# One signal of TensorE per expert tile, two banks and a third weight buffer in a fused attention and mixture-of-experts block

## The chip, the cores and the metric

The kernel runs on one core of a Trainium2 chip. The metric is the device time of one execution in microseconds; the kernel before has a median of 491.53 over three runs (491.47 to 492.46). On a core five engines run their own instruction streams: TensorE (PE, with its weight loads as PEld), VectorE (DVE), ScalarE (ACT), GpSimd (POOL) and SyncE (SP). They meet only at semaphores: an instruction adds one when it is done, another waits until a count is reached. SP, ACT and POOL also issue DMAs.

## What is computed

The block takes 16 sequences of 256 positions with 128 features. A modulated layer norm feeds a linear attention with a state that is updated position by position (the scan), its result is gated and added to the input; a second modulated layer norm feeds a mixture of eight experts, of which each position takes one:

```python
h = _layernorm(x, axis=-1) * (1 + ca) + sa
x = x + ga * _L0_attn_ref(h, ...)          # the scan over 256 positions
h = _layernorm(x, axis=-1) * (1 + cb) + sb
x = x + gb * _L0_ffn_ref(h, ...)
...
logits = x @ router_w + router_b
max_ind = jnp.argmax(route, axis=1)
for e in range(num_experts):               # 8 experts
    a, g = jnp.split(x @ w1[e], 2, axis=1) # 128 -> 2 x 512
    y = jax.nn.silu(a) * g @ w2[e]         # 512 -> 128
    out = jnp.where((max_ind == e)[:, None], y, out)
out = out * max_prob
```

## The kernel before

The positions are cut in two halves of 128. Up to about 300 us the scan runs on DVE, with the other engines beside it. The first half's rows go through the router while the scan of the second half still runs; the second half's only after it.

The experts' stage is what the change touches. For each half POOL scatters the 2048 normed rows into a DRAM array sorted by expert (`sort_rows`, L996, 16 indirect DMAs of 128 rows each, in three bursts of 6, 5 and 5, each burst waiting for the one before it to land). The sorted rows form 23 tiles of 128 rows with one expert each (`NF = 23`), so 46 tiles, g = 0 to 45. What each engine does for a tile:

- SP loads the tile's rows (L534), after the whole half has been scattered.
- PE turns the rows (`turn_x`, L827, one product against the identity, into bank 0), makes the first products in two halves of eight (`hidden`, L839), and two tiles later the second products, eight (`second`, L854, into bank 3). Its loop over g is: first half of `hidden(g)`, `turn_x(g + 2)`, second half of `hidden(g)`, `second(g - 2)`.
- DVE copies the turned rows to SBUF (`xst`, L1886) and their places (L1888), multiplies (`gate_u`, L1893), and from tile 13 on copies the result (`ys`, L1900).
- ACT applies the silu (L1386), copies the next but one tile's first weights into one of two buffers (`copy_w1`, L1399), and up to tile 12 copies the result (`ys`, L1406).
- POOL scatters the result rows (L1052), after tile 10 stops for the second half's `sort_rows` (`SCAT = 10`), and then goes on with tile 11.

Every order is written out by hand. PE counts four kinds of event apart: `xt_ps` for each turn, `h_ps` for each half of `hidden`, `y_ps` for each `second`. So it signals four times in a tile. The silu starts at the first half's signal, `xst` at the turn's, `copy_w1` at the second half's.

While tiles 3 to 15 run, other work of the second half is woven in: PE adds `attend` (L710) behind tiles 3 and 4, turns of normed rows (L729) behind 8 and 10, router products and turns back (L738, L747) behind 9 and 11, and the ranks (L755) behind 12. On DVE, behind `xst` of the same iteration, stand the statistics, the scaling, `shift2` (L1796, eight instructions at 9 and 11, which PE's router products wait for), the routing (L1727 to L1739 at 12, which the ranks wait for) and the sorted places (L1759 to L1785 at 13, which POOL's `sort_rows` waits for). `scale_outputs` (L246) follows `gate_u` in iterations 0 and 1; ACT sends what the first one made by four DMAs (L259) before it copies tile 3's weights.

## Time and profile before

| what | us |
|---|---|
| median of the runs (lowest, highest) | 491.53 (491.47, 492.46) |
| span of the profiled execution, first to last instruction | 487.9 |
| PE busy in the span | 377.1 (77%) |
| DVE busy | 383.3 (79%) |
| ACT busy | 277.9 (57%) |
| POOL busy | 263.1 (54%) |
| chain that ended last, by engine | DVE 33%, PE 31%, POOL 13%, issue 11% |
| mean granted TensorE clock | 0.886 of full speed |

For the profiled execution only its span is known; the median of the runs is 3.6 us above it. The page's second part cuts the span in 40 slices: PE shows 9 in nearly all of the slices from 404 us to 470 us, and in that stretch the chain that ended last is PE's products, tile after tile. From 370 us to 404 us the same chain is broken by pieces called "issue" and "another core or an unknown queue", that is, time for which the profile shows no releaser or one that it can't name. Before 300 us the chain is DVE's scan.

### The profile page before, as it was taken

The page shows a single profiled execution, that of the slowest core. Times are in us where ns is not written, and L with a number is a line of the kernel's source. Part 1 is how long each engine was busy: PE and PEld are TensorE (multiplying, and loading weights), DVE is VectorE, ACT ScalarE, POOL GpSimd, SP SyncE. Part 2 cuts the span into 40 slices and gives each one's busy share as a digit, 9 for nine tenths or more (in the row PEclk, how much of TensorE's full clock was granted, in tenths as well). Part 3 has the DMA queues.
Part 4 walks back from the last instruction along what each step waited for, and adds up shares of the span by engine and source line. Part 5 has one row for each costly group of instructions (what it writes and reads, how often), then busy time and mean ns, then how long its engine had stood idle before and what let it go on. Part 6 is the DMA issues. An engine that isn't in the chain of part 4 may idle for free.

```text
span 487.9 us, 8633 instructions
## 1 busy us (share of the span) xinstructions
PE 377.1 (77%) x2505; PEld 325.1 (67%) x2505; DVE 383.3 (79%) x1166; ACT 277.9 (57%) x624; POOL 263.1 (54%) x325
## 2 busy tenths in 40 slices
PE   2967763956799978948779588699997779999970
PEld 1322312754678568938669578598997678999960
DVE  5778999999999999999979997749664224468624
ACT  3697967756474666766466353548454354555520
POOL 1127238999999678576772884022216663333340
PEclk9978995978889997987976869989999977999995
DMA  8177799990000019431000011341131122414006
GB/s 227 41 101 125 109 118 151 103 69 1 1 0 1 2 18 388 114 57 31 0 2 0 13 39 51 75 88 35 39 114 38 50 78 56 130 42 130 29 27 177
DMA packets 49309, 35.00 MB, mean 72 GB/s; under 512 B 10992, under 2 KB 45584, under 8 KB 49136
## 3 DMA queue, kind: packets, MB, share of 16 engines
q1 hardware_dynamic: 45424, 28.28, 30.7%
q0 software_dynamic: 3264, 5.92, 4.0%
q8 instruction: 21, 0.34, 0.3%
q10 hardware_dynamic: 576, 0.26, 0.2%
q14 instruction: 24, 0.20, 0.2%
HBM read 15.26 MB, written 10.27 MB: 52 GB/s over the span
## 4 chain that ended last, share of the span: by engine, by line
DVE 33%; PE 31%; POOL 13%; issue 11%; ACT 5%; DMA 2%; another core or an unknown queue 2%; ACTq 1%; SPq 0%; POOLq 0%; DVEq 0%
PE bank L839 12%; PE bank L854 5%; DVE U L1682 5%; DVE S L1695 5%; DVE p L1676 4%; DVE p L1689 4%; PE bank L650 4%; POOL big L950 2%; DVE big L1612 2%; PE bank L738 2%; DVE X L1614 2%; PE bank L593 1%; PE bank L654 1%; POOL X L918 1%
## 5 line engine op out<-in xcount | busy, mean ns | idle before, releaser
L1052 POOL DMA_INDIRECT placed_y<-Q,place x46 | 44.1, 958 | 101.9 <-DVE place L1888 38.1
L839 PE MATMUL bank<-Q,p 128*128 128x128 f32 x736 | 97.2, 281 | 2.2 <-ACT p L1399 2.2
L650 PE MATMUL bank<-prod_o,ID 128*128 128x128 f32 x512 | 75.4, 308 | 29.0 <-POOL prod_o L294 17.1
L839 PEld LDWEIGHTS bank<-Q,p 128*128 128x128 f32 x736 | 92.1, 197 | 2.6 <-ACT p L1399 2.4
L650 PEld LDWEIGHTS bank<-prod_o,ID 128*128 128x128 f32 x512 | 70.4, 219 | 31.8 <-POOL prod_o L294 20.3
L1210 ACT ACTIVATE p<-S,GAM 128x64 f32<-128x64 f32 x126 | 48.3, 410 | 65.4 <-DVE S L1695 64.6
L287 POOL TENSOR_TENSOR prod_o<-Q,ST 128x1024 f32<-128x1024 f32 x28 | 60.0, 2141 | 29.6 <-PE bank L654 17.1
L1399 ACT ACTIVATE p<-big 128x1024 f32 x46 | 48.5, 1057 | 44.4 <-PE bank L839 30.7
L1695 DVE TENSOR_REDUCE S<-p 128x64 f32<-128x320 f32 x126 | 56.6, 488 | 0.0
L1682 DVE TENSOR_REDUCE U<-p 128x32 f32<-128x288 f32 x128 | 53.0, 454 | 0.0
L1676 DVE TENSOR_TENSOR p<-S,bank 128x256 f32<-128x256 f32 x128 | 49.7, 423 | 0.7 <-ACT bank L1205 0.7
L1689 DVE TENSOR_TENSOR p<-U,bank 128x256 f32<-128x256 f32 x126 | 48.4, 423 | 0.0
L854 PE MATMUL bank<-big,S 128*128 x248 | 34.7, 284 | 9.6 <-issue 4.6
L996 POOL DMA_INDIRECT sorted_h<-X,pos x32 | 30.9, 965 | 18.6 <-issue 8.1
L593 PE MATMUL bank<-ph,WP 128*128 128x512 f32 x48 | 29.9, 772 | 13.4 <-ACT ph L1098 13.4
L854 PEld LDWEIGHTS bank<-big,S 128*128 128x128 f32 x248 | 30.7, 195 | 11.3 <-issue 11.2
L1893 DVE TENSOR_TENSOR S<-S,bank 128x512 f32<-128x512 f32 x31 | 21.3, 687 | 19.1 <-PE bank L839 11.0
L654 PEld LDWEIGHTS bank<-prod_o,ID 128*128 128x128 f32 x256 | 35.2, 213 | 0.0
L654 PE MATMUL bank<-prod_o,ID 128*128 128x128 f32 (+3 forms) x256 | 34.7, 284 | 0.0
L1886 DVE COPY Q<-bank 128x128 f32<-128x128 f32 x46 | 13.3, 288 | 27.1 <-PE bank L827 21.7
L294 POOL TENSOR_TENSOR prod_o<-PD,U 128x128 f32<-128x128 f32 (+1 forms) x112 | 33.7, 339 | 0.0
L1386 ACT ACTIVATE S<-bank 128x512 f32<-128x512 f32 x31 | 18.5, 595 | 20.0 <-PE bank L839 10.0
(253 smaller groups left out, 740.4 us busy)
## 6 DMA issues: line engine op xcount, KB each, us to landing
big<-in_L_ffn_w_dram SPq DMA_DIRECT2D x1, 4096.0 KB, 14.1
big<-big SPq DMA_DIRECT2D x16, 192.0 KB, 5.0
Q<-sorted_h SPq DMA_DIRECT2D x46, 64.5 KB
sorted_h<-ZERO SPq DMA_DIRECT2D x2, 1472.0 KB, 19.4
X<-in_L_attn_x_dram SPq DMA_DIRECT2D x8, 256.0 KB, 4.4
big<-big SPq DMA_DIRECT2D x16, 128.0 KB, 5.2
K<-placed_y SPq DMA_DIRECT2D x8, 256.0 KB
out_dram<-X SPq DMA_DIRECT2D x8, 256.0 KB, 2.3
```

Of the source, the lines that this page charges most:

```text
L287: engine.tensor_tensor(slot[:, 0:HD, :, :, :], q, states.unsqueeze(3).broadcast_to(full), ALU.mult)
L650: pe.matmul(ps, ID[:, :], prod_o[:, k % 2, i, :], start=(i == 0), stop=False, skip_group_check=True)
L654: m = pe.matmul(o4, ID[:, :], r4, start=False, stop=(d == C - 1), skip_group_check=True)
L839: m = pe.matmul(bank[(1, 6)[g % 2] + k][:, c * P:(c + 1) * P], W1E[g % 2][:, f:f + P], XST[:, g % 3, :], start=True, stop=True)
L854: m = pe.matmul(bank[3][:, 0:D], GU[g % 3][:, c * P:(c + 1) * P], W2[:, bass.ds(expert, 1), c, :], start=(c == 0), stop=(c == FC - 1))
L1052: pool.indirect_dma_start(placed_y[g // NF], bass.IndirectOffsetOnAxis(ap=place[:, g:g + 1], axis=0), YS[:, g % YR, :], None).then_inc(sem ...
L1210: act.activation(p2[h][:, :, :, C], S_[h][:, n % SR, :, :], ACT.Copy, scale=GAM[h][:, n:n + 1])\
L1399: act.activation(W1E[g % 2].unsqueeze(1), W1[:, bass.ds(expert, 1), :], ACT.Copy).then_inc(sem("w1_copied"), 1)
L1676: dve.tensor_tensor(p1[h][:, n % UR, :, :, 0:HD], s_, w, ALU.mult).then_inc(sem("seq_w", h), 1)
L1682: dve.tensor_reduce(U_[h][:, n % VR, :, :], p1[h][:, n % UR, :, :, :], AX_X, ALU.add)\
L1689: dve.tensor_tensor(p2[h][:, :, :, 0:C], u, k, ALU.mult).then_inc(sem("state_in", h), 1)
L1695: dve.tensor_reduce(S_[h][:, (n + 1) % SR, :, :], p2[h][:, :, :, :], AX_X, ALU.add).then_inc(sem("s_ready", h), 1)
```

## The change

PE signals once per tile, at its last product, on one count `tile_ps`; `xt_ps`, `h_ps` and `y_ps` go. The helpers `hidden_done`, `result_done` and `turned` translate a tile to that count. From tile 17 on (`WIDE = 16`) turned rows alternate between banks 0 and 5 and results between banks 3 and 4, and PE waits for the copy of the last but one instead of the last. First weights get a third buffer from tile 8 on, and ACT copies them three tiles ahead from iteration 5 on, in which it copies two. DVE's `ys` moves from three iterations behind to two, and behind `xst`.

```diff
+        W1E.append(flatq[0][:, HB * P:HB * P + F2])
+        THREE, WIDE = 6, F_ROUTE + 4
+        def first_weights(g):
+            return W1E[g % 2 if g < THREE else (g - THREE) % 3]
+        def hidden_done(g):
+            return g + 3 if g < NF else g + 7
+        def result_done(g):
+            return g + 5 if g < NF else hidden_done(g + 2)
+        def turned(g):
+            if g < 2:
+                return g + 1
+            return g + 5 if NF <= g < NF + 2 else hidden_done(g - 2)
+        def turned_bank(g):
+            return bank[5 if g > WIDE and g % 2 else 0][:, 0:P]
+        def result_bank(g):
+            return bank[4 if g > WIDE and g % 2 else 3][:, 0:D]
...
             def turn_x(g):
                 pe.wait_ge(sem(f"xs_in{g % XR}"), 16 * (g // XR + 1))
                 if g >= 1:
-                    pe.wait_ge(sem("xst_ready"), g)
-                pe.transpose(bank[0][:, 0:P], XS[:, g % XR, 0:D], ID[:, :]).then_inc(sem("xt_ps"), 1)
+                    pe.wait_ge(sem("xst_ready"), g if g <= WIDE else g - 1)
+                if g == WIDE + 1:
+                    pe.wait_ge(sem("h2_evac"), 8)
+                return pe.transpose(turned_bank(g), XS[:, g % XR, 0:D], ID[:, :])
...
-                    m.then_inc(sem("h_ps"), 1)
                     if k == 0 and g + 2 < G and g + 2 not in (NF, NF + 1):
                         turn_x(g + 2)
+                return m
...
                 if g >= 1:
-                    pe.wait_ge(sem("ys_ready"), g)
+                    pe.wait_ge(sem("ys_ready"), g if g <= WIDE else g - 1)
+                if g == WIDE + 1:
+                    pe.wait_ge(sem("pos_ready"), 2)
...
-                m.then_inc(sem("y_ps"), 1)
+                return m
...
                 if g < G:
-                    hidden(g)
+                    last = hidden(g)
                 if g >= 2 and g not in (NF, NF + 1):
-                    second(g - 2)
+                    last = second(g - 2)
+                last.then_inc(sem("tile_ps"), 1)
...
             def silu(g):
-                act.wait_ge(sem("h_ps"), 2 * g + 1)
-                if g >= 3:
-                    act.wait_ge(sem("y_ps"), g - 2)
+                act.wait_ge(sem("tile_ps"), hidden_done(g))
...
-                if g >= 2:
-                    act.wait_ge(sem("h_ps"), 2 * (g - 1))
-                else:
+                if g < 2:
                     act.wait_ge(sem("u_ready", g), NCH)
+                if g == THREE + 2:
+                    act.wait_ge(sem("ot_in0_", 1), 16 * HB)
...
-                if g + 2 < G:
+                if g < THREE:
                     copy_w1(g + 2)
+                if THREE - 1 <= g and g + 3 < G:
+                    copy_w1(g + 3)
...
             def xst(g):
-                dve.wait_ge(sem("xt_ps"), g + 1)
-                if g >= 3:
-                    dve.wait_ge(sem("h_ps"), 2 * (g - 2))
-                dve.tensor_copy(XST[:, g % 3, :], bank[0][:, 0:P]).then_inc(sem("xst_ready"), 1)
+                dve.wait_ge(sem("tile_ps"), turned(g))
+                dve.tensor_copy(XST[:, g % 3, :], turned_bank(g)).then_inc(sem("xst_ready"), 1)
...
             def gate_u(g):
                 dve.wait_ge(sem("silu_a"), g + 1)
-                dve.wait_ge(sem("h_ps"), 2 * g + 2)
...
-                elif g >= YACT + 3 and g not in (NF + 1, NF + 2):
-                    if g == YACT + 3:
-                        dve.wait_ge(sem("ys_ready"), YACT)
-                    ys(g - 3)
                 if g + 2 < G and g + 2 not in (NF, NF + 1):
                     xst(g + 2)
+                if g >= YACT + 2 and g not in (NF, NF + 1):
+                    if g == YACT + 2:
+                        dve.wait_ge(sem("ys_ready"), YACT)
+                    ys(g - 2)
```

DVE's program around iterations 12 and 13 of the kernel before, with the semaphores that each instruction waits for: the multiply of tile 11, then the copy of tile 14's turned rows, and the start of the routing.

```order
L1893 TENSOR_TENSOR S<-S,bank 128x512 [waits h_ps,silu_a]
L1886 COPY Q<-bank 128x128 [waits h_ps,xt_ps]
L1888 CAST place<-Q 128x1 [waits xs_in0]
L1727 TENSOR_TENSOR RT<-bank,RB 128x128 [waits lg_ps]
L1732 TENSOR_REDUCE lmx<-RT 128x16 [waits dve_link]
```

The same place in the changed kernel:

```order
L1927 TENSOR_TENSOR S<-S,bank 128x512 [waits silu_a]
L1921 COPY Q<-bank 128x128 [waits tile_ps]
L1923 CAST place<-Q 128x1 [waits xs_in0]
L1763 TENSOR_TENSOR RT<-bank,RB 128x128 [waits lg_ps]
L1768 TENSOR_REDUCE lmx<-RT 128x16 [waits dve_link]
```

Nothing changes its place here; the copy of the turned rows, which stands ahead of the routing, now waits for the count of whole tiles.

DVE's program of iterations 16 and 17 before: multiply of tile 15, result of tile 13, turned rows of tile 18, multiply of 16, result of 14.

```order
L1893 TENSOR_TENSOR S<-S,bank 128x512 [waits h_ps,silu_a]
L1900 COPY Q<-bank 128x128 [waits ys_out0,y_ps,ys_ready]
L1886 COPY Q<-bank 128x128 [waits h_ps,xt_ps]
L1888 CAST place<-Q 128x1 [waits xs_in4]
L1893 TENSOR_TENSOR ST<-ST,bank 128x512 [waits h_ps,silu_a]
L1900 COPY Q<-bank 128x128 [waits ys_out1,y_ps]
```

And in the changed kernel, from the multiply of tile 15 on:

```order
L1927 TENSOR_TENSOR S<-S,bank 128x512 [waits silu_a]
L1921 COPY Q<-bank 128x128 [waits tile_ps]
L1923 CAST place<-Q 128x1 [waits xs_in4]
L1934 COPY Q<-bank 128x128 [waits ys_out1,tile_ps]
L1927 TENSOR_TENSOR ST<-ST,bank 128x512 [waits silu_a]
```

The result's copy now stands behind the turned rows, and it is one tile further on: `ys_out1` is tile 14's, one iteration earlier than before.

## Rows read from the trace of the kernel before

**Rows 1.** Busy time by stretch (engines' busy us, then PEclk, DMA share, GB/s).

```profile
369.70:404.70 35.00, 26.21 (x191) 24.65 (x190) 9.33 (x27) 15.29 (x18) 22.26 (x24) 0.90 0.19 58
391.00:394.00 3.00, 3.00 (x16) 3.00 (x16) 1.06 (x4) 2.04 (x3) 1.98 (x3) 0.50 0.45 114
```

**Rows 2.** Timeline of PE, tile 5 (start us, us, engine, line, operation, [idle before]).

```profile
328.40 1.06 PE L839 MATMUL bank<-Q,p 128*128 128x128 f32 x8
329.29 0.27 PE L827 MATMUL bank<-ID,Q 128*128 128x128 f32 x1
...
331.19 1.06 PE L839 MATMUL bank<-Q,p 128*128 128x128 f32 x8
```

**Rows 3.** Timeline of ACT and DVE in the same tile.

```profile
329.49 0.60 ACT L1386 ACTIVATE S<-bank 128x512 f32<-128x512 f32 x1 [1.73 <-PE bank L839]
329.60 0.29 DVE L1886 COPY Q<-bank 128x128 f32<-128x128 f32 x1 [1.35 <-PE bank L827]
...
333.00 0.69 DVE L1893 TENSOR_TENSOR S<-S,bank 128x512 f32<-128x512 f32 x1
```

**Rows 4.** Timeline of all engines during POOL's first burst, tiles 15 to 17.

```profile
366.71 0.96 POOL L996 DMA_INDIRECT sorted_h<-X,pos  x1 [4.60 <-DVE pos L1785]
...
370.61 0.27 PE L827 MATMUL bank<-ID,Q 128*128 128x128 f32 x1
...
373.02 0.96 POOL L996 DMA_INDIRECT sorted_h<-X,pos  x1 [0.31 <-issue]
...
374.55 1.15 PE L854 MATMUL bank<-big,S 128*128 x8 [2.77 <-issue]
...
375.43 0.60 ACT L1386 ACTIVATE ST<-bank 128x512 f32<-128x512 f32 x1 [2.75 <-remote]
375.47 0.29 DVE L1886 COPY Q<-bank 128x128 f32<-128x128 f32 x1 [1.18 <-remote]
```

**Rows 5.** Timeline during a burst of the first half's sort, before the experts' stage.

```profile
295.45 0.96 POOL L996 DMA_INDIRECT sorted_h<-X,pos  x1 [1.61 <-DMA sorted_h<-X,pos]
...
298.20 0.98 PE L654 MATMUL bank<-prod_o,ID 128*128 128x128 f32 x8
...
299.21 0.28 ACT L1240 ACTIVATE K<-bank 128x128 f32<-128x128 f32 x1 [3.77 <-PE bank L654]
```

**Rows 6.** Timeline of DVE, SP and PE: from places to the second half's first turn.

```profile
366.26 0.17 DVE L1785 CAST pos<-bank 128x16 uint32<-128x16 f32 x1
...
391.16 0.32 SPq L534 DMA_DIRECT2D Q<-sorted_h  x1
...
404.73 0.42 PE L827 MATMUL bank<-ID,Q 128*128 128x128 f32 x1
...
302.93 0.36 SPq L534 DMA_DIRECT2D Q<-sorted_h  x1
...
304.86 0.30 PE L827 MATMUL bank<-ID,Q 128*128 128x128 f32 x1
```

**Rows 7.** Timeline of PE and DVE: places in tiles 3 to 13 where PE waits.

```profile
317.52 1.16 PE L839 MATMUL bank<-Q,p 128*128 128x128 f32 x8 [2.25 <-ACT p L1399]
...
339.95 1.15 PE L854 MATMUL bank<-big,S 128*128 x8 [1.12 <-ACT Q L1406]
...
354.09 1.06 PE L738 MATMUL bank<-RW,K 128*128 128x8 f32 x8
...
360.56 0.49 PE L755 MATMUL bank<-RT,LOWER 128*128 128x128 f32 x2 [0.68 <-DVE RT L1739]
...
362.55 0.29 DVE L1886 COPY Q<-bank 128x128 f32<-128x128 f32 x1 [1.45 <-PE bank L827]
```

**Rows 8.** Timeline of PE: tile 20 and the last products.

```profile
389.83 1.37 PE L854 MATMUL bank<-big,S 128*128 x8 [1.86 <-issue]
...
469.23 1.06 PE L854 MATMUL bank<-big,ST 128*128 x8
...
472.62 1.15 PE L854 MATMUL bank<-big,S 128*128 x8 [0.59 <-DVE Q L1900]
```

More of the change, by code:

```diff
@@ L838, in hidden @@
                         f = (k * FC + c) * P
-                        m = pe.matmul(bank[(1, 6)[g % 2] + k][:, c * P:(c + 1) * P], W1E[g % 2][:, f:f + P], XST[:, g % 3, :],
+                        m = pe.matmul(bank[(1, 6)[g % 2] + k][:, c * P:(c + 1) * P], first_weights(g)[:, f:f + P], XST[:, g % 3, :],
                                       start=True, stop=True)
-                    m.then_inc(sem("h_ps"), 1)
                     if k == 0 and g + 2 < G and g + 2 not in (NF, NF + 1):
                         turn_x(g + 2)
+                return m
             def second(g):
@@ L851, in second @@
                 if g >= 1:
-                    pe.wait_ge(sem("ys_ready"), g)
+                    pe.wait_ge(sem("ys_ready"), g if g <= WIDE else g - 1)
+                if g == WIDE + 1:
+                    pe.wait_ge(sem("pos_ready"), 2)
                 for c in range(FC):
-                    m = pe.matmul(bank[3][:, 0:D], GU[g % 3][:, c * P:(c + 1) * P], W2[:, bass.ds(expert, 1), c, :],
+                    m = pe.matmul(result_bank(g), GU[g % 3][:, c * P:(c + 1) * P], W2[:, bass.ds(expert, 1), c, :],
                                   start=(c == 0), stop=(c == FC - 1))
-                m.then_inc(sem("y_ps"), 1)
+                return m
             for g in range(2):
-                turn_x(g)
+                turn_x(g).then_inc(sem("tile_ps"), 1)
             for g in range(G + 2):
@@ L862, in _ @@
                     for k in (2, 1):
-                        second(g - k)
+                        second(g - k).then_inc(sem("tile_ps"), 1)
                     for k in range(2):
-                        turn_x(g + k)
+                        turn_x(g + k).then_inc(sem("tile_ps"), 1)
                 if g < G:
-                    hidden(g)
+                    last = hidden(g)
                 if g >= 2 and g not in (NF, NF + 1):
-                    second(g - 2)
+                    last = second(g - 2)
+                last.then_inc(sem("tile_ps"), 1)
                 if g in F_ATTEND:
@@ L1393, in copy_w1 @@
                     act.wait_ge(sem("tex_ready"), s + 1)
-                if g >= 2:
-                    act.wait_ge(sem("h_ps"), 2 * (g - 1))
-                else:
+                if g < 2:
                     act.wait_ge(sem("u_ready", g), NCH)
+                if g == THREE + 2:
+                    act.wait_ge(sem("ot_in0_", 1), 16 * HB)
                 expert = act.value_load(tex[s][0:1, j:j + 1], min_val=0, max_val=E - 1)
-                act.activation(W1E[g % 2].unsqueeze(1), W1[:, bass.ds(expert, 1), :], ACT.Copy).then_inc(sem("w1_copied"), 1)
+                act.activation(first_weights(g).unsqueeze(1), W1[:, bass.ds(expert, 1), :], ACT.Copy).then_inc(sem("w1_copied"), 1)
             def ys(g):
-                act.wait_ge(sem("y_ps"), g + 1)
+                act.wait_ge(sem("tile_ps"), result_done(g))
                 if g >= YR:
                     act.wait_ge(sem(f"ys_out{g % YR}"), 16 * (g // YR))
-                act.activation(YS[:, g % YR, :], bank[3][:, 0:D], ACT.Copy).then_inc(sem("ys_ready"), 1)
+                act.activation(YS[:, g % YR, :], result_bank(g), ACT.Copy).then_inc(sem("ys_ready"), 1)
             for h in range(NHALF):
@@ L1896, in ys @@
             def ys(g):
-                dve.wait_ge(sem("y_ps"), g + 1)
+                dve.wait_ge(sem("tile_ps"), result_done(g))
                 if g >= YR:
                     dve.wait_ge(sem(f"ys_out{g % YR}"), 16 * (g // YR))
-                dve.tensor_copy(YS[:, g % YR, :], bank[3][:, 0:D]).then_inc(sem("ys_ready"), 1)
+                dve.tensor_copy(YS[:, g % YR, :], result_bank(g)).then_inc(sem("ys_ready"), 1)
             def finish(s, q):
@@ L1923, in _ @@
             xst(1)
-            for g in range(G + 3):
+            for g in range(G + 2):
                 if g == NF:
-                    for k in (3, 2, 1):
+                    for k in (2, 1):
                         ys(g - k)
```

## Prediction

> **What bounds the kernel now.** I read the chain that ended last first. From 404 us on it is PE's products, one tile after another, up to the scatters and stores of the end; between 370 and 404 us it breaks into pieces without a known releaser. Then the busy times by stretch: from 369.7 to 404.7 us PE is busy 26.2 of 35.0 us [rows 1]. The timeline of an undisturbed tile says what this stretch should take. Tile 5 begins at 328.40, its turn at 329.29, tile 6 at 331.19 [rows 2]: eight products take 0.89 us, the turn 0.11, a whole tile (24 products and the turn) 2.79. The stretch holds tiles 16 to 22, two of them without a turn, and two second products: 7 × 2.79 − 0.22 + 1.78 = 21.1 us. So 13.9 of the 35.0 us are lost there, to waits and to half clock.
>
> The timelines of all engines show what the waits are. In tile 5 ACT begins its silu at 329.49 and DVE its copy at 329.60, each 0.20 us after the last product that it needs [rows 2, 3]. In tile 16 the first half ends at 370.61 and the turn at 370.72, but ACT's silu and DVE's copy start together at 375.43 and 375.47 [rows 4], some 4.7 us late, and neither waits for anything else in the program that is still running. PE itself then waits 2.77 us, because the result that DVE has to copy was late in the same way. POOL was issuing six indirect DMAs back to back, from 366.71 to 373.98; the two start 1.5 us after the last. The same pattern comes back in the next three bursts. I take it that PE's signals arrive late while POOL issues in bursts. But not always: in a burst of the first half's sort, running since 295.45, PE ends its eight products of L654 at 298.20 + 0.89 = 299.1, and ACT follows at 299.21 [rows 5]. There PE signals once in 24 products, here four times in 25. So what fits both is that signals pile up when they are close together. This is an inference, not something that a row says.
>
> A second path runs beside PE's. The places of the second half are ready at 366.26 + 0.17 = 366.43; POOL's sixteen scatters follow, and SP loads the first sorted tile at 391.16, which is 24.73 us later [rows 6]. In the first half the turn came 304.86 − 302.93 = 1.93 us after that load. So tile 23's turn could have stood at 393.09; PE, held up, came to it at 404.73. There are 11.6 us between what the sort allows and what PE did.
>
> **The change, part by part.** *One signal per tile.* In tiles 16 to 22 signals then come 2.79 us apart, about as far as in rows 5. I count these waits as gone, with 1.9 us of cover left in any case: the silu of tile g is needed at the start of tile g + 2, 2.79 us after the signal, and takes 0.20 + 0.60 [rows 3].
>
> *The price of the one signal.* DVE's copy of turned rows moves from the turn's end to the tile's end, from 329.40 to 331.19 [rows 2], or 1.79 us. Whatever stands behind that copy on DVE and is waited for by PE or POOL moves as well:
> - Tile 0 has no second products, so there the move is one group of eight, 0.89. Behind the copy stand the square roots, `gate_u`, `scale_outputs`, then ACT's four DMAs and the copy of tile 3's weights, for which PE already waits 2.25 us [rows 7]: +0.89.
> - Iteration 5: from the copy at 329.60 DVE works without a gap on the statistics; ACT's root and result copy follow, and PE already waits 1.12 us for that at 339.95 [rows 7]: +1.79. The wait that ACT's two weight copies in iteration 5 make for PE a tile or two earlier (about 1 us) lies inside this.
> - Iterations 9 and 11: PE's router products began at 354.09 with no idle time worth a note beside the row [rows 7], just as the first four of DVE's `shift2` were done; with 0.1 us of slack that is +1.7 each, 3.4 in all.
> - Iteration 12: the ranks already wait 0.68 us for DVE's routing [rows 7]: +1.79.
> - Iteration 13: the copy at 362.55 [rows 7] stands ahead of the sorted places: +1.79.
>
> The places are then 0.89 + 1.79 + 3.4 + 1.79 + 1.79 = 9.7 us later, at 376.1, and tile 23's turn at 376.1 + 24.73 + 1.93 = 402.8. PE gets there sooner: it begins tile 15's second half at 377.0, when the multiply behind the places (0.69 [rows 3]) is done, ends tile 15 two groups later at 378.8, and with 21.1 us of work and 0.9 of waiting for the last multiply ends both second products at 400.8. So 2 us of delays could return there for nothing, and the sort is the bound. Against 404.73: −1.9.
>
> *Two banks.* After the turn of tile 23 the next turn no longer waits for DVE's copy (−0.3), two short waits of some 0.2 us each while DVE runs the first half's end go (−0.4), and at the very end the last second products, which wait 0.59 at 472.62 after a like wait just before, start when the multiply is done: tile 45 ends at 469.23 + 0.89 = 470.12 [rows 8], +0.20, silu 0.60, multiply 0.69 [rows 3], +0.2 is 471.8, so −0.8. Together −1.5. In tiles 25 to 43 PE already runs without a gap, so the banks give nothing there.
>
> *The third buffer* lets the weights arrive a tile earlier; where PE runs gap-free nothing waits for them, so nothing. *Fewer signals on PE:* the turn follows a signalled product 0.11 us after the group's end, as any product follows another [rows 2], so nothing. The Trainium skill, in "TensorE: Matmul & The Clock Gate", section "The cost: per-tile semaphore tail", gives some 26 ns to each increment and says that one on the last product is enough. By that the 138 signals that go would be worth an estimated 3.6 us, and the sum would be that much lower; tile 5's rows show no such time.
>
> *The clock.* From 391 to 394 us the granted clock is 0.50, the lower of TensorE's two levels (1.2 and 2.4 GHz), and 16 products fill 3.0 us [rows 1] instead of 1.8: 1.2 us lost there, and 1.7 over the whole fall, which began a little earlier. It followed PE's 1.86 us wait at 389.83 [rows 8], yet not the longer one of 2.77 us at 374.55 [rows 4]. The change makes three new waits of this length before the places, 1.8 in iterations 9 and 11 and 2.5 at the ranks. Between no fall and three (0 to 5.1 us) I take one: +1.7.
>
> **The sum.** −1.9 − 1.5 + 1.7 = −1.7 us on the span of 487.9, which gives 486.2. The median of the runs is 3.6 us above that span, and I keep this distance: 491.53 − 1.7 = **489.8**.
>
> **The rivals.** A measurement of this kernel can tell about 0.2%, 1 us, from no change.
>
> *Signals are held by the burst itself* (slower). If POOL's back-to-back issue holds any signal of PE until it pauses, then one signal per burst passes, and PE, two tiles deep, does two tiles per burst. A burst and its pause took about 7.5 us, so 3.8 us a tile: tiles 16 to 22 and the second products end at 378.8 + 28 = 407, or 4 us after the sort's bound, and while POOL then works off the waiting results for some 16 us, four tiles lose 1 us each. 489.8 without the clock term is 488.1; plus 8 is 496. For it: the late starts fall 1 to 1.5 us after bursts. Against it: rows 5. It decides as soon as signals arrive more than 1.9 us late.
>
> *The clock falls at every new wait* (slower). 491.53 − 3.4 + 5.1 = 493.2. For it: the wait of 1.86 us; against: the one of 2.77.
>
> *The early waits are partly hidden* (faster). If ACT or DVE have more slack in iterations 5 to 13 than the rows of PE's waits show and only half of the 9.7 us appears, the turn of tile 23 moves to 398 and the time to about 484. Against it: at each of these places PE or POOL already waits, or is within 0.1 us of waiting.
>
> *Signals cost PE time* (faster). If each signal that goes gave PE back its spacing, the time would fall further; rows 2 are rounded to 0.01, so three signals in 46 tiles can give at most 1.4 us: 488.4. This is what the page's rule would come to here.
>
> **How the numbers follow.** The forecast, with no fall of the clock (488.1), one (489.8) or two (491.5), has 0.60, 0.20 each. Held signals 0.18, three falls 0.12, half the early waits 0.07, signals that cost 0.03. Faster by over 0.2% are the first two of the forecast and the last two rivals: 0.40 + 0.07 + 0.03 = 0.50. Same is the third of the forecast, 0.20. Slower are the held signals and three falls, 0.30. The forecast's own range is 487 to 492. The 8-in-10 range runs from 486.5, which leaves out the hidden waits, to 496, up to the held signals at their price.
>
> **What would show it.** Right: in the second half's sort, silu and copy start about 0.2 us after a tile's end; PE's router products, twice, and the ranks wait some 2 us; the places come near 376 us, SP's first load near 401, tile 23's turn near 403, and that turn waits for the load, not for PE. The last second products follow a wait for the multiply, not for a result's copy. Wrong: starts that still come a microsecond after a burst; a turn of tile 23 that follows PE's products without a wait; places before 372 or after 380 us.

## The result and the profile after

The changed kernel takes 502.81 us (median of four runs, 500.54 to 506.5) against 491.5 for the kernel before: 1.0267 of its time, interval 1.0219 to 1.0314. It is slower by 11.3 us; I had forecast 1.7 us less, and a range that ended at 496.0.

The profiled execution of after has a span of 498.8 us and a time of 500.54; that of before 487.9. The difference of the spans, 10.9 us, is what the two traces have to account for. Every reading below is of one profiled execution per kernel.

The page of after, its first part and two groups of its fifth (busy us, mean ns of one | idle us before, and what ended most of it):

```profile
span 498.8 us, 8511 instructions
PE 379.7 (76%) x2505; PEld 327.3 (66%) x2505; DVE 382.1 (77%) x1166; ACT 277.9 (56%) x624; POOL 263.3 (53%) x325
...
L1921 DVE COPY Q<-bank 128x128 f32<-128x128 f32 x46 | 13.3, 289 | 65.2 <-PE bank L888 50.7
...
L1420 ACT ACTIVATE S<-bank 128x512 f32<-128x512 f32 x31 | 18.5, 596 | 49.0 <-PE bank L888 40.8
```

The same two groups on the page of before:

```profile
L1886 DVE COPY Q<-bank 128x128 f32<-128x128 f32 x46 | 13.3, 288 | 27.1 <-PE bank L827 21.7
...
L1386 ACT ACTIVATE S<-bank 128x512 f32<-128x512 f32 x31 | 18.5, 595 | 20.0 <-PE bank L839 10.0
```

The work is the same to within 3 us on each engine. What grew is idle time: DVE is now idle for 65.2 us ahead of its copies of turned rows where it was idle for 27.1, and 50.7 us of that end with the last product of a tile; ahead of ACT's silu it is 49.0 us where it was 20.0. In before some of that idle time was no loss to anybody, so the groups alone don't say what the program lost. That stands in PE's timeline, at the places of [rows 7]. After, PE, tiles 3 to 13, rows with a wait of over 1 us, and the next tile's products behind the last three:

```profile
320.14 1.16 PE L871 MATMUL bank<-Q,p 128*128 128x128 f32 x8 [2.24 <-ACT p L1433]
...
330.60 2.02 PE L739 MATMUL bank<-ph,X 128*128 128x128 f32 x16 [1.20 <-DVE X L1755]
...
338.50 1.15 PE L888 MATMUL bank<-big,ST 128*128 x8 [1.20 <-ACT Q L1440]
...
346.36 1.15 PE L888 MATMUL bank<-big,S 128*128 x8 [1.50 <-ACT Q L1440]
...
352.89 1.06 PE L767 MATMUL bank<-RW,K 128*128 128x8 f32 x8 [1.72 <-DVE K L1832]
...
356.67 1.92 PE L871 MATMUL bank<-Q,p 128*128 128x128 f32 x8
...
366.06 1.06 PE L767 MATMUL bank<-RW,K 128*128 128x8 f32 x8 [1.72 <-DVE K L1832]
...
368.90 1.74 PE L871 MATMUL bank<-Q,p 128*128 128x128 f32 x8
...
375.95 0.79 PE L784 MATMUL bank<-RT,LOWER 128*128 128x128 f32 x2 [2.46 <-DVE RT L1775]
...
377.01 1.89 PE L871 MATMUL bank<-Q,p 128*128 128x128 f32 x8
```

In before the same stretch shows three waits, 2.25, 1.12 and 0.68 us [rows 7]. Soon after each of the last three waits a row of eight products takes 1.7 to 1.9 us instead of 1.06. Busy time by stretch of after shows why (columns as in [rows 1]; the clock stands before the DMA share):

```profile
357.00:358.30 1.30, 1.30 (x8) 1.30 (x8) 0.00 (x0) 0.52 (x1) 0.00 (x0) 0.50 0.00 0
369.20:370.40 1.20, 1.20 (x7) 1.20 (x7) 0.00 (x0) 0.50 (x1) 0.00 (x0) 0.50 0.00 0
...
377.20:378.60 1.40, 1.40 (x8) 1.40 (x8) 0.00 (x0) 0.00 (x0) 0.00 (x0) 0.50 0.88 351
```

The granted clock is 0.50, the lower level of 1.2 GHz. In before it was full throughout:

```profile
340.00:366.70 26.70, 26.02 (x224) 25.24 (x225) 17.76 (x62) 13.42 (x23) 5.72 (x6) 1.00 0.23 70
```

The second path, from the places to the second half's first turn, in after (DVE, POOL, SP and PE):

```profile
384.81 0.17 DVE L1821 CAST pos<-bank 128x16 uint32<-128x16 f32 x1
...
385.26 0.96 POOL L1031 DMA_INDIRECT sorted_h<-X,pos  x1 [8.54 <-DVE pos L1821]
...
409.22 2.70 SPq L563 DMA_DIRECT2D Q<-sorted_h  x6
...
418.27 0.64 PE L859 MATMUL bank<-ID,Q 128*128 128x128 f32 x2
```

Counted from the stage's first turn (306.61, and 304.86 before), the places are ready after 78.37 us instead of 61.57: 16.8 later. The load follows them by 24.2 us, before by 24.7 [rows 6]. But tile 23's turn follows the load by 9.05 us, not by 1.93, and without any wait for it: PE came late. A burst shows what held it. After, second half's sort, ACT, PE, POOL and DVE around the end of the first burst:

```profile
387.85 0.60 ACT L1420 ACTIVATE S<-bank 128x512 f32<-128x512 f32 x1 [1.58 <-issue]
...
389.54 1.06 PE L888 MATMUL bank<-big,S 128*128 x8
...
391.58 0.96 POOL L1031 DMA_INDIRECT sorted_h<-X,pos  x1 [0.30 <-issue]
393.89 0.60 ACT L1420 ACTIVATE ST<-bank 128x512 f32<-128x512 f32 x1 [4.20 <-remote]
393.89 0.29 DVE L1921 COPY Q<-bank 128x128 f32<-128x128 f32 x1 [4.04 <-remote]
...
394.70 1.15 PE L888 MATMUL bank<-big,S 128*128 x8 [2.10 <-DVE Q L1934]
```

The signal of the tile that ended at 387.64 arrived in 0.21 us. The next tile ended at 389.54 + 0.89 = 390.43; ACT and DVE saw it together at 393.89, 3.46 us later and 1.35 us after POOL's last issue of the burst ("remote" stands for a releaser that the profile can't name). The longest delays in the other two bursts are 2.90 and 3.92 us. So one signal per tile is held like four. PE's busy time from the first indirect DMA to tile 23's turn, before and after:

```profile
366.71:404.73 38.02, 29.23 (x219) 27.67 (x217) 11.76 (x36) 17.04 (x21) 24.67 (x26) 0.90 0.19 57
...
385.26:418.27 33.01, 25.30 (x207) 24.09 (x206) 11.48 (x36) 15.20 (x20) 21.07 (x22) 0.98 0.19 57
```

PE is idle for 7.7 us there instead of 8.8. Most of the 5.0 us by which this piece is shorter is busy time: PE starts it about 12 products further on, and the granted clock is 0.98 instead of 0.90.

The end is as forecast in kind. After, PE, last products:

```profile
473.75 1.06 PE L871 MATMUL bank<-Q,p 128*128 128x128 f32 x8
...
476.54 1.95 PE L871 MATMUL bank<-Q 128*128 128x128 f32 x16
...
483.58 1.15 PE L888 MATMUL bank<-big,S 128*128 x8 [0.62 <-DVE S L1927]
```

The last wait is for the multiply, and a tile still takes 476.54 - 473.75 = 2.79 us. From tile 23's turn to POOL's last scatter it is 67.1 us instead of 69.7: 2.6 gained. The account: the stage began 1.75 us later (nothing of the change lies before it; it is the spread of runs), 16.8 later places, 418.27 - 384.98 = 33.3 us from there to the turn instead of 38.3 (-5.0), -2.6 at the end: 10.95, and the spans differ by 10.9.

### The profile page after: what moved, and what is told of

Its sections match the earlier page's. It is cut to its first block and busy times, and to the rows that moved or that the text cites. A ratio compares the mean times of both kernels' runs of the same rounds, so it can differ in the third digit from the quotient of the medians.

```text
span 498.8 us, 8511 instructions
## 1 busy us (share of the span) xinstructions
PE 379.7 (76%) x2505; PEld 327.3 (66%) x2505; DVE 382.1 (77%) x1166; ACT 277.9 (56%) x624; POOL 263.3 (53%) x325
## 5 line engine op out<-in xcount | busy, mean ns | idle before, releaser
L679 PEld LDWEIGHTS bank<-prod_o,ID 128*128 128x128 f32 x512 | 70.4, 219 | 33.0 <-POOL prod_o L323 21.6
L871 PE MATMUL bank<-Q,p 128*128 128x128 f32 x528 | 72.3, 287 | 4.4 <-ACT p L1433 2.2
L871 PEld LDWEIGHTS bank<-Q,p 128*128 128x128 f32 x528 | 68.2, 203 | 5.1 <-ACT p L1433 2.4
L1921 DVE COPY Q<-bank 128x128 f32<-128x128 f32 x46 | 13.3, 289 | 65.2 <-PE bank L888 50.7
L1712 DVE TENSOR_TENSOR p<-S,bank 128x256 f32<-128x256 f32 x128 | 48.5, 407 | 0.7 <-ACT bank L1240 0.7
L1725 DVE TENSOR_TENSOR p<-U,bank 128x256 f32<-128x256 f32 x126 | 47.3, 407 | 0.0
L622 PE MATMUL bank<-ph,WP 128*128 128x512 f32 x48 | 32.0, 821 | 14.6 <-ACT ph L1133 14.5
L1433 ACT ACTIVATE p<-big 128x1024 f32 x33 | 34.7, 1056 | 7.2 <-issue 6.3
L888 PE MATMUL bank<-big,S 128*128 x248 | 33.6, 278 | 5.0 <-DVE Q L1934 2.1
L683 PEld LDWEIGHTS bank<-prod_o,ID 128*128 128x128 f32 x256 | 36.4, 219 | 0.0
L683 PE MATMUL bank<-prod_o,ID 128*128 128x128 f32 (+3 forms) x256 | 35.9, 290 | 0.0
L622 PEld LDWEIGHTS bank<-ph,WP 128*128 128x128 f32 x48 | 11.7, 261 | 30.8 <-ACT ph L1133 16.5
```

Of the source, the lines that this page charges most:

```text
L622: m = pe.matmul(bank[1 + i][:, :], WP[:, i, :], rhs, start=True, stop=True)
L679: pe.matmul(ps, ID[:, :], prod_o[:, k % 2, i, :], start=(i == 0), stop=False, skip_group_check=True)
L683: m = pe.matmul(o4, ID[:, :], r4, start=False, stop=(d == C - 1), skip_group_check=True)
L871: m = pe.matmul(bank[(1, 6)[g % 2] + k][:, c * P:(c + 1) * P], first_weights(g)[:, f:f + P], XST[:, g % 3, :], start=True, stop=True)
L888: m = pe.matmul(result_bank(g), GU[g % 3][:, c * P:(c + 1) * P], W2[:, bass.ds(expert, 1), c, :], start=(c == 0), stop=(c == FC - 1))
L1712: dve.tensor_tensor(p1[h][:, n % UR, :, :, 0:HD], s_, w, ALU.mult).then_inc(sem("seq_w", h), 1)
```

## The experiments

Two questions: is the loss made before the places or after, and what holds the signals? The table has, for each kernel, three pieces of its trace: from the stage's first turn to the first indirect DMA of the second half's sort (A), from there to tile 23's turn (B), and from that turn to POOL's last scatter (C); beside B stand PE's idle time and the mean granted clock in it. Times are medians in us; "before" is the kernel before on the same chip, the ratio has its 95% interval.

| kernel | A | B | idle in B | clock in B | C | time | before | ratio |
|---|---|---|---|---|---|---|---|---|
| before | 61.9 | 38.0 | 8.8 | 0.90 | 69.7 | 491.5 | | |
| changed | 78.7 | 33.0 | 7.7 | 0.98 | 67.1 | 502.81 | 491.5 | 1.0267 (1.0219 to 1.0314) |
| late14 | 60.3 | 34.6 | 7.2 | 0.97 | 66.9 | 482.89 | 488.95 | 0.9878 (0.9796 to 0.9961) |
| four_banks | 61.9 | 30.1 | 3.4 | 1.00 | 68.1 | 481.85 | 488.95 | 0.9860 (0.9784 to 0.9936) |
| one_nobanks | 77.9 | 36.6 | 10.5 | 0.94 | 68.6 | 503.99 | 488.95 | 1.0296 (1.0215 to 1.0376) |
| late14_pre | 65.2 | 28.1 | 1.4 | 1.00 | 72.6 | 487.63 | 488.95 | 0.9973 (0.9934 to 1.0012) |
| turn14 | 62.7 | 40.9 | 11.6 | 0.87 | 67.6 | 492.60 | 494.74 | 0.9970 (0.9936 to 1.0005) |
| late14_reads | 62.7 | 34.8 | 6.9 | 0.94 | 67.5 | 486.84 | 494.74 | 0.9866 (0.9793 to 0.9939) |
| late14_narrow | 61.9 | 41.7 | 15.7 | 0.87 | 70.8 | one run | 494.74 | |
| late14_threes | 61.9 | 31.0 | 6.2 | 0.94 | 71.8 | 486.21 | 494.74 | 0.9839 (0.9780 to 0.9899) |
| turn14_threes | 64.2 | 31.0 | 5.7 | 0.96 | 70.8 | 487.71 | 493.38 | 0.9895 (0.9861 to 0.9929) |
| late14_fours | 61.9 | 29.3 | 3.9 | 1.00 | 68.5 | 479.95 | 493.38 | 0.9739 (0.9664 to 0.9814) |
| four_fours | 60.2 | 28.5 | 3.3 | 1.00 | 68.7 | 480.44 | 493.38 | 0.9766 (0.9686 to 0.9847) |
| before_threes | 61.9 | 32.7 | 7.2 | 0.97 | 74.8 | 487.82 | 493.38 | 0.9890 (0.9818 to 0.9962) |

The kernel before differs by 1.2% between the sets, so kernels of different sets are compared by ratio. A, B and C come from one execution each. Kernels with the same program up to the places (late14, late14_threes and late14_fours) have an A of 60.3 to 61.9: in late14 the granted clock stayed full at tile 3, where it fell to the lower level in the other two. It stayed full there in turn14 and four_fours as well, and fell in before and changed. In the kernels with bursts of three, 4.9 to 5.3 us of the idle time in B are the wait for the load.

### Where the loss is made

**late14** keeps the four signals up to iteration 13 (`LATE = 14`). The core of the edit (the waits on the other engines follow it):

```diff
+                    if g < LATE:
+                        m.then_inc(sem("h_ps"), 1)
...
+                        if g < LATE:
+                            r.then_inc(sem("xt_ps"), 1)
...
-                last.then_inc(sem("tile_ps"), 1)
+                if g >= LATE:
+                    last.then_inc(sem("tile_ps"), 1)
+                elif g >= 2:
+                    last.then_inc(sem("y_ps"), 1)
```

> The changed kernel, but with the four signals of before in iterations 0 to 13 of TensorE's loop, one per tile from 14 on; banks, third buffer and the order of the result copies as changed. Theory A (the loss is made before the places: DVE's copy of turned rows, held back to the tile's end, delays all that stands behind it): the places come as early as before, PE's waits at the router products and ranks go back to 0 to 0.7 us, and from the first indirect DMA to tile 23's turn it takes the 33.0 us of the changed kernel (38.0 before): 491.5 - 5.0 - 2.6 (tail) = 484, range 482 to 487. Theory B (the loss comes from what the change does from tile 14 on: banks, order of the copies, signals held in POOL's bursts): no better than 497.

**four_banks** is the same with `LATE = 1000`: four signals to the end, so only banks, third buffer and the earlier result copy are left of the change.

> Four signals per tile throughout, as before; only the two banks each, the third weight buffer and the earlier result copy of the change are kept. Theory A: places as early as before, PE held in POOL's bursts as before (38 us from the first indirect DMA to tile 23's turn, less up to 2 where the second bank lets PE run ahead), tail 1.5 to 2.6 shorter: 487 to 490. Theory B: some of the loss is here, 493 or more.

**one_nobanks** keeps the one signal and the earlier result copy, without the banks and the third buffer:

```diff
-        THREE, WIDE = 6, F_ROUTE + 4
+        THREE, WIDE = 1000, 1000
```

> One signal per tile as changed, but one bank each for turned rows and results and two weight buffers throughout. Theory A: the places are as late as in the changed kernel (about 385 us), the tail is 1.5 to 2.6 us longer: 503 to 506. Theory B (banks or third buffer cost the time): under 498.

Theory A holds in all three: with one signal before the places the kernel is 3% slower, banks or no banks; without it, it is 1.2 to 1.4% faster than before. In late14 A falls from 78.7 to 60.3 us, and PE waits 0.68 us for the ranks and not at all at the router products. The banks, the buffer and the earlier result copy together are worth 1.4% (interval 0.6 to 2.2%); I had expected 0.3 to 0.9%, with up to 2 us in the bursts, where B falls by 8, from 38.0 to 30.1 us: 5.4 us less idle time, the rest at a granted clock of 1.00 instead of 0.90. One signal instead of four from tile 14 on shows no gain over that.

**turn14** asks which waiter makes the loss. Everything waits for the tile's end as changed, but up to iteration 13 the turn signals as well, and DVE's copy waits for that (`TURNS = 14`):

```diff
+                        if g < TURNS:
+                            r.then_inc(sem("xt_ps"), 1)
...
-                dve.wait_ge(sem("tile_ps"), turned(g))
+                if g - 2 < TURNS:
+                    dve.wait_ge(sem("xt_ps"), g + 1)
+                    if g >= 3:
+                        dve.wait_ge(sem("tile_ps"), g - 2)
```

> The changed kernel with one signal more: up to iteration 13 the turn signals by itself too, and DVE's copy of turned rows waits for that; everything else waits for the tile's end as changed. Theory A1 (as the prediction had it: DVE's copy of turned rows is what makes the loss before the places): places 60 to 62 us after the stage's first turn, as before (changed kernel 78.4), time as with four signals up to iteration 13, 481 to 485. Theory A2 (the silu, the result's copy and the weight copies, which start at the tile's end as well, share in the loss): places after more than 64 us, 487 or more.

The places come 62.4 us after the first turn: A1 in the main. But in this trace the clock did not fall at tile 3, as it did in before and in changed. In turn14_threes (below), whose program is the same up to the places, it did, and there the places come after 63.9 us. Like for like, 78.4 - 63.9 = 14.5 of the 16.8 us belong to the one copy that stands ahead of other work on DVE, with the falls of the clock that follow it. The late silu and result copies, which still make PE wait for the results of tiles 4 to 6 (1.20, 0.25 and 1.50 us), have the other 2.3, the share that A2 spoke of. The time that A1 gave did not come either: B took 40.9 us, more than in any other kernel of full rows. From iteration 14 on its program is late14's, yet PE is idle for 11.6 us there instead of 7.2, and the granted clock is lower. late14 and turn14, B:

```profile
365.27:399.88 34.61, 27.40 (x219) 25.85 (x218) 11.62 (x36) 16.42 (x21) 22.40 (x24) 0.97 0.19 58
...
369.67:410.57 40.90, 29.30 (x222) 27.73 (x222) 11.74 (x36) 16.42 (x21) 25.16 (x27) 0.87 0.18 54
```

What differs is where its tiles end in the bursts. turn14, second burst, which began at 378.58, and the end:

```profile
380.56 1.06 PE L891 MATMUL bank<-big,S 128*128 x8
...
383.64 0.96 POOL L1037 DMA_INDIRECT sorted_h<-X,pos  x1 [0.30 <-issue]
385.90 0.60 ACT L1431 ACTIVATE S<-bank 128x512 f32<-128x512 f32 x1 [4.96 <-remote]
...
386.71 1.65 PE L891 MATMUL bank<-big,ST 128*128 x6 [3.19 <-DVE Q L1962]
```

A tile ended at 381.45, and its signal was seen at 385.90; PE waited 3.19 us. So the way through the bursts looks like a lottery: with one signal per tile it takes 28 to 41 us in kernels whose tile 15 begins between 1.05 us before the first indirect DMA (changed) and 1.0 after it (late14_pre below).

### What holds the signals

**late14_pre** reads the experts of tiles 14 to 22 into registers ahead of the bursts, since PE's own register reads could be what the bursts hold up:

```diff
+                if g == 12:
+                    for i in range(14, 23):
+                        pe_expert[i] = pe.value_load(tex[0][0:1, i:i + 1], min_val=0, max_val=E - 1)
```

> As the kernel with four signals up to iteration 13, and TensorE reads the experts of tiles 14 to 22 into registers in iteration 12, before POOL's bursts, instead of one ahead of each tile's second products. Theory H1 (POOL's back-to-back indirect DMAs by themselves hold PE's signals): ACT and DVE still start 2 to 4 us late in the bursts, time within 1.5 us of the kernel without the early reads. Theory H2 (PE's register read is held up by the bursts, and its signals behind it; in the first half's bursts, where PE reads no register, signals pass within 0.25 to 0.7 us): starts 0.2 us after a tile's end, tile 23's turn set by the sort, 26.7 us after the places: 5 to 7 us faster than that kernel.

Undecided by the time: the reads in one place made the ranks wait 4.40 us, so the sort began later, and B was the shortest of all (28.1). The signals were late all the same, by up to 2.87 us, but PE was idle for only 1.4 us in B; C is 5.7 us longer than late14's. **late14_reads** spreads them over waits of tiles 0 to 3:

```diff
+                if g == 3:
+                    read_experts(range(18, 23))
...
+                    if k == 0 and g in (0, 2):
+                        read_experts(range(14 + g, 16 + g))
```

> Four signals up to iteration 13, one from 14 on; TensorE reads the experts of tiles 14 to 22 into registers in waits that it has anyway, in tiles 0 to 3 (two, two and five reads). The first try of this, with all nine reads in iteration 12, made the ranks wait 4.4 us, but shortened the way from the first indirect DMA to tile 23's turn from 34.6 to 28.1 us. H2 (register reads in the bursts hold TensorE's signals): places as early as with four signals, 28 us to the turn: 475 to 479. H1 (the bursts by themselves): 33 us or more, 481 to 485.

B is 34.8 us, as in late14, and a signal is up to 4.46 us late: H2 falls. late14_pre's short B was then, as far as one trace tells, luck of the same lottery. late14_reads, PE in the bursts:

```profile
382.31 1.15 PE L901 MATMUL bank<-big,ST 128*128 x8 [1.41 <-issue]
...
391.28 3.37 PE L878 MATMUL bank<-Q,p 128*128 128x128 f32 x16 [1.95 <-issue]
```

**late14_narrow** scatters one number per row into an array of its own; the second half's experts then work on padding rows.

```diff
-                    pool.indirect_dma_start(sorted_h[s], bass.IndirectOffsetOnAxis(ap=pos[s][:, t:t + 1], axis=0),
-                                            H2[s][t // HB][:, t % HB, :], None).then_inc(sem("scattered", s), 16)
+                    c = slice(0, 1) if s else slice(0, D1)
+                    pool.indirect_dma_start(narrow if s else sorted_h[s], bass.IndirectOffsetOnAxis(ap=pos[s][:, t:t + 1], axis=0),
+                                            H2[s][t // HB][:, t % HB, c], None).then_inc(sem("scattered", s), 16)
```

> Four signals up to iteration 13, one from 14 on; the second half's sort scatters one number of each row (4 bytes) instead of 129 into an array of its own, with as many indirect DMAs in the same bursts; the second half's experts then work on padding, and the result isn't the reference's. Theory T (what the DMAs move holds TensorE's signals): ACT and DVE start 0.2 us after a tile's end in the bursts. Theory I (POOL's issue or the number of descriptors holds them): starts 1.3 to 3 us late as before. The time says little, since the bursts may land sooner.

late14_narrow, PE, ACT and POOL in and after the first burst, which began at 368.90:

```profile
371.43 1.15 PE L893 MATMUL bank<-big,ST 128*128 x8 [0.26 <-ACT Q L1462]
...
374.64 0.60 ACT L1435 ACTIVATE S<-bank 128x512 f32<-128x512 f32 x1 [3.47 <-remote]
...
375.20 1.07 POOL L1041 DMA_INDIRECT narrow<-X,pos  x1 [0.30 <-issue]
...
381.44 1.06 PE L893 MATMUL bank<-big,ST 128*128 x8
...
382.53 0.60 ACT L1435 ACTIVATE S<-bank 128x512 f32<-128x512 f32 x1 [1.09 <-PE bank L893]
...
383.58 0.95 POOL L1041 DMA_INDIRECT narrow<-X,pos  x1 [7.30 <-DMA narrow<-X,pos]
```

With 4 bytes a row, the tile that ended at 372.41 is still seen 2.23 us late. And after POOL's last issue, while the scatters are still under way until shortly before 383.58 (they take longer, not less), the tile that ended at 382.33 is seen in 0.20 us, and so is the one before it. So, in this one trace, it is POOL's issuing that goes with late signals, not transfers in flight, nor the bytes. What of the issuing does it (the descriptors, their number, POOL's own writes) stays open.

**late14_threes** cuts the bursts:

```diff
+    BURSTS1 = (0, 3, 6, 9, 12, 14, NT)
...
-                first, end = BURSTS[burst:burst + 2]
+                first, end = (BURSTS1 if s else BURSTS)[burst:burst + 2]
```

> Four signals up to iteration 13, one from 14 on; the second half's sort in six bursts (3, 3, 3, 3, 2, 2) instead of three (6, 5, 5), each waiting for the one before to land. Sort longer by three pauses of 1.3 us, about 4 us: first load of sorted rows 28 us after the places. If signals are held only from some 2.4 us after a burst's start until it lands: no wait of PE over 1 us there, tile 23's turn set by the load, 30.5 us after the places (34.8 before): 478 to 480. If they are held whatever the length of the burst: turn 35 us or more after the places, 483 to 488.

late14_threes, first burst (369.16 to 372.65) and tile 23's turn:

```profile
371.69 1.15 PE L892 MATMUL bank<-big,ST 128*128 x8 [0.26 <-issue]
...
373.51 0.60 ACT L1432 ACTIVATE S<-bank 128x512 f32<-128x512 f32 x1 [2.08 <-PE bank L892]
...
400.13 0.92 PE L859 MATMUL bank<-ID,Q 128*128 128x128 f32 x2 [5.31 <-DMA Q<-sorted_h]
```

The tile that ends at 372.67 is seen 0.84 us later; in all four bursts of three the delay stays below 0.9, PE's longest wait is 0.62, and the turn waits 5.31 us for the load. Now the sort is the bound, as the prediction had it. The gain is smaller than expected: 0.9839 is not clear of late14's 0.9878. B is 3.6 us shorter, but C is 5.0 longer. The held signals come back after the turn, while POOL works off waiting results in runs of five: a tile that ended at 410.40 was seen at 413.38.

**turn14_threes, late14_fours, four_fours and before_threes** put the same edit on four kernels; the two with bursts of four also pause after every third result (`range(SCAT + 3, NF + 2, 3)` for `(SCAT + 5, SCAT + 10)`).

> The kernel with the turn's own signal up to iteration 13 (places as early as before, yet 0.997 of the time before), with the second half's sort in bursts of 3, 3, 3, 3, 2, 2. Theory P (what that kernel lost after the places, 40.9 us from the first indirect DMA to tile 23's turn, is signals held while POOL issues; in a burst of three they are held at most 0.9 us, less than TensorE's slack): turn after 31 us, set by the load, ratio to before 0.980 to 0.988. Theory Q (something else in tiles 14 to 22 is slow with that signal): turn after 36 us or more, ratio above 0.992.

> Four signals up to iteration 13, one from 14 on; sort in bursts of four, and POOL also pauses after every third waiting result instead of every fifth. In bursts of three (ratio 0.9839) the turn waited 5.3 us for the load, so TensorE was done some 25.7 us after the first indirect DMA. Theory P: the load comes 25.5 us after it, signals are held at most 3 us with 1.9 us of slack, the turn at 27.5 to 28.5, and the waits after it for results held in runs of five go: ratio 0.974 to 0.981. If a burst of four already holds signals as long as one of six: turn at 32 or more, 0.984 to 0.990.

> Four signals per tile throughout, with the banks and the third buffer, sort in bursts of four and results in runs of three. With the long bursts: 0.986 of before, turn of tile 23 at 30.1 us after the first indirect DMA. Theory P as for the kernel with one signal from 14 on, and four signals cost nothing by themselves: turn at 27.5 to 28.5, ratio 0.974 to 0.981. If signals pile up when they are close together (the prediction's reading): one signal is better here, and this one stays at 0.984 or above.

> The kernel before with one edit: the second half's sort in bursts of 3, 3, 3, 3, 2, 2. Theory P: turn of tile 23 at 31 us after the first indirect DMA instead of 38.0, places and tail as before: ratio 0.984 to 0.988. If its four signals per tile are what makes them late: turn at 35 or later, ratio 0.993 to 1.0.

Theory P holds for B: turn14's falls from 40.9 to 31.0 us, the kernel before's from 38.0 to 32.7, each with one edit in POOL's program and none in PE's signals. Their turns now wait 4.86 and 4.97 us for the load. Both ratios are a little above what I expected, because C is longer: PE waits for held results later (turn14_threes 1.80 us at 415.67). In the trace of before_threes, its slowest execution, C takes back 5.1 of the 5.3 us, so its gain of 1.1% stands on the times alone. late14_fours' turn came after 29.3 us, a little later than expected. four_fours and late14_fours don't differ beyond their intervals: I see no part that the number of signals plays. **late14_fours** has the lowest ratio, 0.9739 of the kernel before. A better one would, I think, keep at least the turn's signal up to the places, the banks, and short bursts; I have not built it.

I did not try bursts of three or four on the changed kernel itself.

## Why the prediction was wrong

**"The price of the one signal", 9.7 us: the mechanism was right, the size was not.** DVE's copy does move what stands behind it (turn14 and turn14_threes give this copy 14.5 us), but the places moved by 16.8 us, 12.5 without the clock. Place by place, as steps of the difference between PE's starts in the two traces:

| place | forecast | measured |
|---|---|---|
| tile 0 | 0.89 | 0.87 |
| tiles 3 to 6 | 1.79 | 3.79 |
| router products, twice | 3.4 | 4.15 |
| ranks | 1.79 | 1.87 |
| iteration 13 | 1.79 | 1.79 |
| clock after the three waits | in "the clock" | 4.33 |

In tiles 3 to 6 I took the one wait that PE already had, at 339.95 [rows 7], and let it grow by the move. I overlooked that `attend` after tile 4 waits for DVE's sum of the first two, which also stands behind the copy: a new wait of 1.20 us, a step of 1.37. The other 2.42 are the results of tiles 4 to 6, for which ACT now has the silu at the tile's end and, in iteration 5, two weight copies ahead.

**"The clock. Between no fall and three I take one": three came**, after exactly the three waits that I had named (1.72, 1.72 and 2.46 us), and they cost 4.33 us where I took 1.7. The steps are 1.41, 1.55 and 1.37 us. I had set the one long wait without a fall [rows 4] against the one with [rows 8]. The length of the wait alone does not settle it: those of 1.20 and 1.50 us were followed by no fall, but neither were those of 2.10 and 1.82 us in the bursts of the same trace, nor late14's of 2.28 us at tile 3, where before's 2.25 us [rows 7] was followed by one (eight products then took 1.62 and 1.91 us). After, first products behind the wait of 1.82 us, and late14, tile 3:

```profile
409.64 2.02 PE L871 MATMUL bank<-Q,p 128*128 128x128 f32 x16 [1.82 <-ACT S L1420]
...
317.71 1.16 PE L870 MATMUL bank<-Q,p 128*128 128x128 f32 x8 [2.28 <-ACT p L1448]
```

What decides whether the clock falls stays open, and the prediction gives no ground for one fall rather than three.

**"I count these waits as gone" fell.** From rows 5 I inferred that signals pile up when they are close together. In the burst of rows 5 there is a second signal that I did not follow: PE's next group ends at 302.1, and ACT starts on it at 302.80, after POOL's last issue and 0.62 us after it was free:

```profile
301.33 0.98 PE L654 MATMUL bank<-prod_o,ID 128*128 128x128 f32 x8
...
302.80 0.28 ACT L1240 ACTIVATE K<-bank 128x128 f32<-128x128 f32 x1 [0.62 <-PE bank L654]
```

Why the signal at 299.1 passed in the middle of its burst stays open. With one signal per tile the changed kernel's bursts hold it for 2.9 to 3.9 us; four_fours beside late14_fours shows no part of the number of signals, and turn14_threes and before_threes show that the length of the bursts matters. So tile 23's turn came 33.3 us after the places, where the sort allows 26.7: 6.6 us. The first rival had this mechanism, with 0.18.

Together: the steps before the places were 2.8 us too small, the clock 2.6, and the bursts 6.6. With the 1.75 us of the later start, and 1.1 less at the end, these 12.6 us lie between the forecast of -1.7 and the 10.9 measured on the spans. The terms that were small had the right sign: the end gave 2.6 us for 1.5 (one_nobanks' C is 1.5 longer than the changed kernel's; the other 1.1 I can't place), and nothing came back in the gap-free tiles. There the tile takes 2.79 us with one signal as with four [rows 2]. The Trainium skill ("TensorE: Matmul & The Clock Gate", "The cost: per-tile semaphore tail") gives some 26 ns to each increment, an estimated 3.6 us for the 138 that go; this trace does not show them.

**The rivals were not exclusive.** I gave held signals 0.18 and three falls 0.12, each with the other's price left out. Both happened; 488.1 + 8 + 5.1 is 501.2, within 1.6 us of the result. A chance for both was missing, and the range had to reach it.

The distance of 3.6 us between the median and the profiled span was a wrong reading too: a fourth run of before, 489.52, lies 1.6 us above that span, and 500.54 lies 1.7 above after's. It was the spread of runs; the difference of the kernels does not hang on it.

## What to carry to other kernels

Before a signal is made coarser, list for each engine that waits for it what stands behind the waiting instruction, and who waits for that; here one copy held up to 1.8 us longer, six times on a chain, and the falls of the clock behind it took most of the 16.8 us by which the places were late, and one extra signal took 14.5 of it away. Where an engine issues indirect DMAs back to back beside a tight loop of TensorE, look at how late the others see TensorE's signals, and try shorter bursts until the delay is below the loop's slack: that alone gave 1.1% here (interval 0.4 to 1.8%), and 2.3% with the banks, the third buffer, the earlier result copy and shorter runs of results (four_fours), of which 1.4% came without the shorter bursts and runs. Rivals that can both come true need a case of their own.

## What the chip showed that I had not expected

TensorE's signals arrive 0.2 us after a tile's end, but up to 4.5 us after it while POOL issues indirect DMAs in bursts of four to six, with 516 bytes a row (4.46 us in late14_reads) as with 4 (2.94 in late14_narrow). In the kernels with one signal per tile in the bursts, most signals in the first 2.4 us of such a burst still pass, though not all: in late14_reads those at 1.34 and 1.69 us were held for 4.46 and 2.66, in late14 one at 1.60 for 1.29. In late14 and four_banks, and once in the changed kernel, TensorE also stops inside a group of products that wait for nothing, and the held signal arrives within 0.2 us after it goes on. late14, PE and ACT at the end of the first burst:

```profile
372.58 0.28 PE L870 MATMUL bank<-Q 128*128 128x128 f32 x1
373.06 0.27 PE L870 MATMUL bank<-Q 128*128 128x128 f32 x1 [0.20 <-issue]
373.77 0.70 PE L870 MATMUL bank<-Q 128*128 128x128 f32 x4 [0.44 <-issue]
373.97 0.60 ACT L1431 ACTIVATE ST<-bank 128x512 f32<-128x512 f32 x1 [2.76 <-remote]
```

In late14_reads and late14_pre, where PE reads no register in the bursts, I found no such stop of 0.2 us or more there, but the late signals all the same. The kernel before and one_nobanks, where it does read them, show no such stop either, so the reads alone don't make it. Whether the products end late or only their signals travel late can't be told, since the profile models the ends of matmuls. The Trainium skill ("Perfetto Trace Analysis", "Tensor Engine Instruction (MATMUL, LD_WEIGHTS)") says that the signal is pushed only when PSUM has acknowledged the writes, after that estimated end; no run here separates the two.

Nor had I expected that two banks help where PE is held: four_banks' B is 8 us shorter than before's with the same signals and the same bursts. In these two traces 5.4 us of it are idle time and the rest is the clock, which stayed full.
